# Five edge aggregations of a graph network: windows of eight steps summed in PSUM, and gather buffers released tile by tile

## Chip, cores and metric

The kernel runs on one core of a Trainium2 chip. The metric is the device time of one execution in microseconds; three runs of the kernel before gave 6568.65, 6569.81 and 6577.09 us (median 6569.81).

## What is computed

There are N = 6250 nodes and E = 100000 edges `(src, dst)`, sorted by `dst`, all with 128 features. The distribution of `dst` is skewed: the first nodes have far more edges. Four layers follow each other, each as `x = x + layer(relu(layernorm(x)))`:

```python
# L0: three graph convolutions
norm = dis[src] * ew * dis[dst]
z = relu(segment_sum((z @ W)[src] * norm[:, None], dst, n) + b)      # three times
# L1: out = x + sum of weighted neighbours, then two dense layers
agg = segment_sum(edge_weight[:, None] * x[src], dst, N)
# L2: attention over the edges, with three segment softmaxes
# L3: mean of neighbours
agg = segment_sum(x[src], dst, N) / maximum(deg, 1)
out = agg @ W_l.T + b_l + x @ W_r.T                                  # then each row is normalised
```

So the same aggregation over all edges is done five times ("passes" 0 to 4): pass 0 to 2 for L0, pass 3 for L1, pass 4, after attention, for L3.

## The kernel before

The nodes lie in 49 blocks of 128 (`NB`), the edges in 782 tiles of 128 (`NT`). The table of node rows to be gathered is in HBM, the sums are in SBUF (`AGG`, one column group of 128 per block).

**Steps.** A tile whose edges go to two blocks is worked twice. A "step" is a pair of a tile and a block; there are `PS = NT + NB - 1` = 830 steps, tile and block both grow with the step, and which tile and block a step has depends on the data. `plan_vector` (L1393) works this out at the start, and the engines read it from `plan_reg` into registers, 16 steps at a time (`load_plan`, L508; `load_blocks`, L513; `load_batches`, L1628).

**A pass** has one program per engine, tied together by semaphores:

- POOL, `gathers` (L748): for each tile one indirect DMA of 128 rows of the table into `gath_ring`, which has `RING` = 64 buffers. At every fourth tile it waits on `freed` for the value of `slot_free(t)` (L420). That value holds for any data: since a step's tile can lag behind its number by up to 48, gather t waits for all steps up to t-13.
- SP, `count_batches` (L526): waits until four gathers have landed and counts them in `landed`.
- VectorE, `sums` (L1635): for each step it makes a one-hot matrix (L1661, 128 edges x 128 nodes of the block, times the edge weight), after waiting every fourth step for the batch that has landed; and it adds the product of an earlier step from PSUM into the block of `AGG` whose number is in a register (L1651 or, with a scale per node, L1653). The adds run up to seven steps behind the one-hots (six banks and one, `lead`, L428).
- TensorE, `products` (L904): for each step two matmuls of 128x512 in bf16 whose result nobody reads (`KEEP_BUSY`, L916), then, after waiting for the one-hot, the fp32 product of one-hot and gathered rows (L918) into one bank of PSUM. Every fourth product counts in `freed`, the others in `multiplied`.

**Between passes.** The last 48 steps of a pass carry the next dense layer with them: from step `NT + STAGE_AT` (6) on, TensorE puts in one stage of `dense_stages` (L866: transposes of one group of four blocks, products of the group before) after every fourth step. ScalarE copies the transposes (`dense_copy`, L1163). From step `NT + DRAIN_AT` (13) on, VectorE drains one group at every fourth step (`gcn_drain`, L1283; `gin_drain`, L1297; `gcn_out`, L1288, from `STAGE_AT`; `sage_drain`, L1371). ScalarE stores the group to the table (`keep_rows`, L1145) and starts `AGG` for the next layer with the node's own row times `dis` (`gcn_start`, L1053). There are 13 groups. The gathers of the next pass wait until all groups of the table are stored.

The order of work is written by hand: each engine's list is the order of the Python program, and nothing is reordered.

## Time and profile before

| what | us |
|---|---|
| median of three runs | 6569.81 |
| the profiled execution: its span, the only time given for it | 7709.4 |
| busy: TensorE matmul | 5132.3 (67%) |
| busy: POOL | 4733.2 (61%) |
| busy: VectorE | 3875.4 (50%) |
| busy: ScalarE | 1090.3 (14%) |
| the 7820 keep-busy matmuls (L916) | 2913.7 |
| the 3910 gathers of the passes (L755) | 3731.9 |
| the 4150 one-hots (L1661) | 1420.2 |
| the 4150 adds (L1651, L1653) | 1402.6 |

The profile is of one execution of the program; its times are from the first to the last instruction. "Idle before" is the time that an engine did nothing ahead of an instruction, with what released it: another engine's line, "issue" where nothing in the trace explains it, "remote" where the semaphore's event came from a source that the trace doesn't name. PE is TensorE's matmuls, PEld its weight loads, DVE VectorE, ACT ScalarE, POOL GpSimd, SP the sync engine. A granted clock of 1.0 is 2.4 GHz, 0.5 is 1.2 GHz. The ends of matmuls are modelled.

### The profile page before, as it was taken

How to read it: one execution, taken by the hardware profiler on the slowest of the kernel's cores; microseconds unless marked ns; L12 is line 12 of the kernel's file. 1: busy time of each engine (PE TensorE's matmuls, PEld its weight loads, DVE VectorE, ACT ScalarE, POOL GpSimd, SP SyncE). 2: the span in 40 equal slices, each digit the busy share in tenths (PEclk: the TensorE clock that was granted, in tenths of full speed). 3: DMA queues.
4: the chain of work that ended last, by engine and by line, in shares of the span. 5: the costliest groups of instructions: out<-in, count | busy, mean ns of one | idle time of the engine just before them, and what ended most of it. 6: DMA issues, size and time to landing. Idle time of an engine off the chain costs nothing.

```text
span 7709.4 us, 94745 instructions
## 1 busy us (share of the span) xinstructions
PE 5132.3 (67%) x25896; PEld 3318.3 (43%) x25896; DVE 3875.4 (50%) x11836; ACT 1090.3 (14%) x3004; POOL 4733.2 (61%) x4806
## 2 busy tenths in 40 slices
PE   2666666666666666666566666678888885666666
PEld 1343444444444434344344443545555553344445
DVE  7444444444444444444533333568888876333334
ACT  2000000100000100000100000256666663000001
POOL 7666666566666466666366666366666644666662
PEclk7777777777777777777677777899999997777777
DMA  2211111211111111111111111155555541111111
GB/s 73 54 46 46 46 46 45 54 46 46 46 46 46 50 46 46 46 46 46 43 46 46 46 46 46 44 123 129 129 130 129 129 105 37 46 46 46 46 46 36
DMA packets 384857, 466.38 MB, mean 60 GB/s; under 512 B 103802, under 2 KB 290616, under 8 KB 384326
## 3 DMA queue, kind: packets, MB, share of 16 engines
q0 software_dynamic: 152528, 313.83, 16.4%
q1 hardware_dynamic: 200936, 128.85, 6.8%
q10 hardware_dynamic: 30878, 17.63, 0.8%
q8 instruction: 225, 3.69, 0.2%
q14 instruction: 290, 2.38, 0.1%
HBM read 434.51 MB, written 27.81 MB: 60 GB/s over the span
## 4 chain that ended last, share of the span: by engine, by line
PE 41%; another core or an unknown queue 21%; issue 15%; DVE 12%; POOL 7%; DVEq 2%; ACT 1%; DMA 0%; SPq 0%; ACTq 0%
PE psum L916 14%; PE psum L918 12%; POOL pool L755 7%; DVE work L1653 5%; PE psum L991 3%; PE psum L956 3%; PE psum L967 3%; PE psum L949 2%; DVE pool L1661 2%; PE psum L891 1%; PE psum L942 1%; PE psum L934 1%; DVEq L1653 1%; DVE work L1651 1%
## 5 line engine op out<-in xcount | busy, mean ns | idle before, releaser
L755 POOL DMA_INDIRECT pool<-table,src_col x3910 | 3731.9, 954 | 2112.6 <-issue 1094.4
L918 PE MATMUL psum<-pool 128*128 x8300 | 2109.2, 346 | 2052.0 <-DVE pool L1661 1376.2
L918 PEld LDWEIGHTS psum<-pool 128*128 128x128 f32 x8300 | 1843.5, 240 | 3358.6 <-issue 3030.4
L916 PE MATMUL psum<-busy_rows,iota_b 128*128 128x512 bf16 x7820 | 2913.7, 461 | 24.1 <-issue 23.7
L1653 DVE SCALAR_TENSOR_TENSOR work<-psum,dis,work 128x128 f32 x2490 | 872.8, 351 | 1732.2 <-remote 1240.4
L1661 DVE TENSOR_SCALAR pool<-iota_f,rel_col,ew_col 128x128 f32<-128x128 f32 x3320 | 1173.9, 354 | 384.5 <-issue 301.7
L916 PEld LDWEIGHTS psum<-busy_rows,iota_b 128*128 128x128 bf16 x7820 | 910.3, 117 | 144.1 <-issue 31.6
L727 POOL DMA_INDIRECT gath<-table,src_col x520 | 518.0, 996 | 325.6 <-PE psum L942 205.2
L1653 DVE SCALAR_TENSOR_TENSOR work<-psum,inv_cnt,work 128x128 f32 x830 | 291.3, 351 | 619.8 <-remote 423.2
L1651 DVE TENSOR_TENSOR work<-work,psum 128x128 f32 x830 | 238.5, 287 | 601.7 <-remote 389.1
L727 POOL DMA_INDIRECT ew_col<-table,src_col x312 | 299.7, 961 | 161.9 <-PE psum L942 82.3
L1171 ACT ACTIVATE pool<-psum 128x512 f32<-128x512 f32 (+1 forms) x104 | 56.4, 563 | 2370.8 <-PE psum L878 2370.8
L956 PE MATMUL psum<-pool,weights 128*128 128x512 f32 x416 | 231.0, 637 | 228.8 <-issue 228.8
L1171 ACT ACTIVATE pool<-psum,gcn_bias 128x512 f32<-128x512 f32 (+1 forms) x26 | 17.1, 660 | 2308.1 <-PE psum L878 2308.1
L1661 DVE TENSOR_SCALAR pool<-iota_f,rel_col 128x128 f32<-128x128 f32 x830 | 246.3, 297 | 82.0 <-issue 67.8
L991 PEld LDWEIGHTS psum<-pool,hot 128*128 128x128 f32 x1664 | 208.6, 197 | 179.7 <-issue 174.2
L1685 DVE TENSOR_TENSOR pool<-psum,pool 128x512 f32<-128x512 f32 x208 | 143.2, 689 | 234.9 <-issue 199.3
L991 PE MATMUL psum<-pool,hot 128*128 128x72 f32 x1664 | 239.1, 286 | 9.7 <-DVE work L1755 5.8
L949 PE MATMUL psum<-pool 128*128 128x128 f32 x1664 | 223.2, 278 | 0.0
L967 PE MATMUL psum<-pool,head_sum 128*32 128x512 f32 x1248 | 221.5, 608 | 1.0 <-DVE pool L1690 1.0
L949 PEld LDWEIGHTS psum<-pool 128*128 128x128 f32 x1664 | 205.6, 194 | 0.0
L1191 ACT ACTIVATE pool<-QV 128x128 f32 x832 | 189.7, 298 | 12.7 <-DVE pool L1763 5.6
(221 smaller groups left out, 3769.3 us busy)
## 6 DMA issues: line engine op xcount, KB each, us to landing
pool<-table,src_col POOLq DMA_INDIRECT x3910
pool<-edge_attr SPq DMA_DIRECT2D x832, 64.0 KB
pool<-step_masks SPq DMA_DIRECT2D x624, 48.0 KB
pool<-rel_rows SPq DMA_DIRECT2D x208, 128.0 KB
table<-work ACTq DMA_DIRECT2D x48, 256.0 KB, 2.3
gath<-table,src_col POOLq DMA_INDIRECT x520
ew_col<-table,src_col POOLq DMA_INDIRECT x312
table<-QV SPq DMA_DIRECT2D x12, 256.0 KB, 2.3
```

The costliest lines, as they stand in the source:

```text
L727: gp.indirect_dma_start(out=q_src(n), out_offset=None, in_=table[0][:, :], in_offset=bass.IndirectOffsetOnAxis(ap=src_col[:, s:s + 1], axis=0)
L755: gp.indirect_dma_start(out=gath_ring[:, t % RING, :], out_offset=None, in_=source[:, :], in_offset=bass.IndirectOffsetOnAxis(ap=src_col[: ...
L916: pe.matmul(psum[:, SUM_BANKS, :], iota_b[:, :], busy_rows[:, :], start=True, stop=True)
L918: pe.matmul(psum[:, steps.bank(s), 0:D], hot_ring[:, s % HOT_RING, :], gath_ring[:, bass.ds(slots[s % REGS], 1), :].rearrange("p a d -> p ...
L949: pe.matmul(psum[:, B_QD, j * P:(j + 1) * P], q_block[:, n % SLOT2, :], expand[:, two, j * P:(j + 1) * P], start=True, stop=True).then_inc ...
L956: pe.matmul(psum[:, B_K, :], weights[:, WI["Wk"], :], attr_t[:, g % 2, :], start=True, stop=True).then_inc(keyed, 1)
L967: ins = pe.matmul(psum[32 * kind:32 * (kind + 1), bank, :], head_sum[:, q, :], prod[:, kind, :], start=(q == 0), stop=(q == QUADS - 1), ti ...
L991: ins = pe.matmul(psum[:, B_SUM, q * ACCW:(q + 1) * ACCW].rearrange("p (k i h) -> p k i h", k=3, i=KINDS), hot[:, two * QUADS + q, :], val ...
L1191: act.activation(q_block[:, slot:slot + 1, :], QV[:, bass.ds(blocks[j], 1), :], ACT.Copy).then_inc(block_copied, 1)
L1651: v.tensor_tensor(into, into, part, ALU.add).then_inc(steps.added, 1)
L1653: v.scalar_tensor_tensor(into, part, scale[:, bass.ds(blocks[added % REGS], 1)], into, ALU.mult, ALU.add).then_inc(steps.added, 1)
L1661: v.tensor_scalar(hot_ring[:, s % HOT_RING, :], iota_f[:, :], rel_col[:, s:s + 1], weight[:, s:s + 1] if weight is not None else None, ALU ...
```

## The change

Steps are put together in windows of `WINDOW` = 8 (104 windows). TensorE sums a window's products in two PSUM banks (8 places of 128 columns): it clears them with two zero matmuls of 128x512, adds each product with `start=False` at the place that a register gives (the step's block less the window's first block), closes with two zero matmuls, and counts the window in `done`. It waits for `landed` itself. VectorE makes the one-hots without waiting for `landed`, into 32 buffers, and adds a whole window (128x1024) at once to eight blocks of `AGG`. The scale by `dis` or `inv_cnt` is applied afterwards, a group at a time. The matmuls that kept TensorE busy are gone.

The gather buffers are 48. For each tile the plan holds the window after which the tile is past (`past_i`); ScalarE waits, batch of four by batch, until that window is done, and counts in `slots_free`, on which POOL waits. The plan gets two more columns (place in the window, first block of the window). `STAGE_AT` goes from 6 to 13, `DRAIN_AT` from 13 to 30.

```diff
-        PLAN = 4
+        PLAN = 6
         PS = NT + NB - 1
+        WINDOW = 8
+        NW = ceil_div(PS, WINDOW)
+        TAIL = NT // WINDOW
...
-        FREE = 4
-        RING = 64
-        HOT_RING = 16
-        SUM_BANKS = PS_BANKS - 1
-        KEEP_BUSY = 2
+        RING = 48
+        HOT_RING = 4 * WINDOW
...
-            def slot_free(self, t):
-                steps = t + FREE - 1 - RING + NB - 1 + 1
-                return self.nth * (PS // FREE) + ceil_div(steps, FREE) if steps > 0 else 0
+            def slots_free(self, t):
+                return self.nth * (TILE_BATCHES - NBATCH) + t // BATCH - NBATCH + 1
+        def window_banks(w):
+            return 2 * (w % 4) if w < TAIL else (2, 6)[(w - TAIL) % 2]
+        def window_lead(w):
+            return 3 if w < TAIL + 2 else 2
+        def last_window(g):
+            return min(NW - 1, (NT + groups[g][1] - 2) // WINDOW)
...
+        def release_slots(act, steps):
+            act.wait_ge(past_loaded, 16)
+            last = TILE_BATCHES - NBATCH
+            for j in range(last):
+                if j % REGS == 0:
+                    n = min(REGS, last - j)
+                    first = BATCH * j + BATCH - 1
+                    past = load_plan(mybir.EngineType.Activation, PLAN, first, (n - 1) * BATCH + 1, NW,
+                                     "a tile's last step is one of PS", BATCH, 1)
+                act.wait_ge(steps.done, past[j % REGS])
+                act.sem_inc(slots_free, 1)
...
-        STAGE_AT = 6
-        DRAIN_AT = 13
+        STAGE_AT = 13
+        DRAIN_AT = 30
...
-                if t % FREE == 0 and t >= RING - NB:
-                    gp.wait_ge(steps.freed, steps.slot_free(t))
+                if t % BATCH == 0 and t >= RING:
+                    gp.wait_ge(slots_free, steps.slots_free(t))
...
-            for s in range(PS):
-                if s < NT:
-                    for _ in range(KEEP_BUSY):
-                        pe.matmul(psum[:, SUM_BANKS, :], iota_b[:, :], busy_rows[:, :], start=True, stop=True)
-                pe.wait_ge(steps.hot, steps.before + s + 1)
-                pe.matmul(psum[:, steps.bank(s), 0:D], hot_ring[:, s % HOT_RING, :],
+            for w in range(NW):
+                if window_before(w) is not None:
+                    pe.wait_ge(steps.added, steps.windows_before + window_before(w) + 1)
+                for k in range(2):
+                    pe.matmul(psum[:, window_banks(w) + k, :], iota_b[:, :], zero_rows[:, :], start=True, stop=False)
+                for s in window_steps(w):
+                    if s % REGS == 0:
+                        slots = load_plan(mybir.EngineType.PE, 2, s, REGS, RING - 1, "the plan takes the tile modulo RING")
+                        places = load_plan(mybir.EngineType.PE, 4, s, REGS, WINDOW - 1, "a step goes on by one block at most")
+                        batches = load_batches(mybir.EngineType.PE, s + BATCH - 1)
+                    if s % BATCH == 0:
+                        pe.wait_ge(landed[steps.nth], batches[s % REGS // BATCH])
+                    pe.wait_ge(steps.hot, steps.steps_before + s + 1)
+                    pe.matmul(window_sums(w)[:, bass.ds(places[s % REGS], 1), :].rearrange("p a d -> p (a d)"),
+                              hot_ring[:, s % HOT_RING, :],
+                              gath_ring[:, bass.ds(slots[s % REGS], 1), :].rearrange("p a d -> p (a d)"), start=False,
+                              stop=False)
+                    if s == window_steps(w)[-1]:
+                        for k in range(2):
+                            ins = pe.matmul(psum[:, window_banks(w) + k, :], iota_b[:, :], zero_rows[:, :], start=False, stop=True)
+                        ins.then_inc(steps.done, 1)
...
+            def add_window(a):
+                v.wait_ge(steps.done, a + 1)
+                into = AGG[:, bass.ds(bases[a % REGS], WINDOW), :]
+                v.tensor_tensor(into, into, window_sums(a), ALU.add).then_inc(steps.added, 1)
+                complete = [g for g in range(NGR) if last_window(g) == a]
+                if ready and complete:
+                    v.wait_ge(steps.added, steps.windows_before + a + 1)
+                    for g in complete:
+                        ready(g)
...
+            while added < NW:
+                if drain and added == NW - 1:
+                    stages = (PS - 1 - NT - STAGE_AT) // GROUP + 1
+                    for g in range(drained, stages - 3):
+                        drain(g)
+                    drained = max(drained, stages - 3)
+                add_window(added)
+                added += 1
+            if drain:
+                for g in range(drained, NGR):
+                    drain(g)
...
+            def scale_sums(col):
+                def scale(g):
+                    lo, hi = groups[g]
+                    v.tensor_tensor(AGG[:, lo:hi, :], AGG[:, lo:hi, :], col_bc(col, lo, hi), ALU.mult).then_inc(sums_scaled, 1)
+                return scale
```

`gcn_start` copies a group without the scale in one operation; `gcn_out` (pass 2) begins with the scale. `release_slots` stands in ScalarE's list ahead of the dense copies of each pass. The plan gets one operation over 1x781, two for `past_i`, about eight of 128x7 and one small matmul.

## Rows read from the trace of the kernel before

**Rows 1.** The span and mean granted clock of the only core.
```profile
core 0: 7709.4 us, clock 0.800
```

**Rows 2.** Instructions of line 755 by stretch: start:end, us; POOL busy (count); granted clock; DMA share; GB/s.
```profile
190.40:1319.40 1129.00, 749.79 (x782) 0.77 0.19 47
1319.40:1385.30 65.90, 0.00 (x0) 0.82 0.23 65
1385.30:2510.30 1125.00, 747.09 (x782) 0.76 0.18 46
...
7593.20:7709.40 116.20, 0.00 (x0) 0.75 0.10 29
```

**Rows 3.** Timeline of POOL: start us, us, what, [idle before <-releaser].
```profile
212.00 0.95 POOL L755 DMA_INDIRECT pool<-table,src_col  x1 [0.31 <-issue]
218.75 0.95 POOL L755 DMA_INDIRECT pool<-table,src_col  x1 [5.80 <-PE psum L918]
...
1030.63 0.95 POOL L755 DMA_INDIRECT pool<-table,src_col  x1 [2.38 <-remote]
1031.89 0.95 POOL L755 DMA_INDIRECT pool<-table,src_col  x1 [0.30 <-issue]
```

**Rows 4.** Waits of POOL from 600 to 1400 us: total us, times, longest us.
```profile
POOL pool L755 <- issue: 143.6, 471, 0.3
POOL pool L755 <- remote: 100.7, 41, 2.6
```

**Rows 5.** Timeline, TensorE at the low and then at the full clock.
```profile
1015.46 0.63 PE L918 MATMUL psum<-pool 128*128 x2
...
1015.88 1.06 PE L916 MATMUL psum<-busy_rows,iota_b 128*128 128x512 bf16 x2
...
1016.74 0.63 PE L918 MATMUL psum<-pool 128*128 x2
...
1022.15 0.38 PE L918 MATMUL psum<-pool 128*128 x2
...
1022.81 0.38 PE L918 MATMUL psum<-pool 128*128 x2
```

**Rows 6.** Timeline, a product and the add that takes it.
```profile
1018.01 0.63 PE L918 MATMUL psum<-pool 128*128 x2
...
1025.57 0.35 DVE L1653 SCALAR_TENSOR_TENSOR work<-psum,dis,work 128x128 f32 x1 [4.33 <-remote]
```

**Rows 7.** Timeline behind the last step of the first pass.
```profile
1379.42 0.35 DVE L1653 SCALAR_TENSOR_TENSOR work<-psum,dis,work 128x128 f32 x1 [0.26 <-PE psum L918]
...
1380.80 0.69 DVE L1286 TENSOR_TENSOR work<-psum,dis 128x512 f32<-128x512 f32 x1 [0.44 <-PE psum L891]
...
1381.85 0.69 DVE L1286 TENSOR_TENSOR work<-psum,dis 128x512 f32<-128x512 f32 x1 [0.35 <-PE psum L891]
...
1385.38 0.97 POOL L755 DMA_INDIRECT pool<-table,src_col  x1 [56.87 <-DMA table<-work]
```

**Rows 8.** Attention: one stretch by engine (PE, PEld, DVE, ACT, POOL; clock, DMA); waits of VectorE.
```profile
5150.00:6300.00 1150.00, 942.89 (x6407) 620.45 (x6405) 947.32 (x2244) 737.92 (x2107) 720.36 (x734) 1.00 0.55 129
...
DVE pool L1685 <- issue: 172.3, 136, 2.4
```

**Rows 9.** Groups of the page, VectorE adds of 128x128 and 128x512 with PSUM.
```profile
L1651 DVE TENSOR_TENSOR work<-work,psum 128x128 f32 x830 | 238.5, 287 | 601.7 <-remote 389.1
...
L1685 DVE TENSOR_TENSOR pool<-psum,pool 128x512 f32<-128x512 f32 x208 | 143.2, 689 | 234.9 <-issue 199.3
```

**Rows 10.** Timeline, repeats of a group's first operation: end of third and of last pass.
```profile
3761.90 0.69 DVE L1291 TENSOR_TENSOR work<-work,bias 128x512 f32<-128x512 f32 x1
...
3767.80 0.68 DVE L1291 TENSOR_TENSOR work<-work,bias 128x512 f32<-128x512 f32 x1
...
7697.48 0.68 DVE L1377 TENSOR_TENSOR pool<-psum,bias 128x512 f32<-128x512 f32 x1
...
7701.00 0.69 DVE L1377 TENSOR_TENSOR pool<-psum,bias 128x512 f32<-128x512 f32 x1 [0.77 <-PE psum L891]
```

More of the change, by code:

```diff
@@ L380, in build @@
         dense_sems = [[sem(f"dense_{k}{side}") for k in ("turned", "copied", "multiplied", "drained")] for side in range(2)]
-        pass_sems = [sem(f"pass_{k}") for k in ("hot", "multiplied", "freed", "added")]
+        pass_hot, pass_added = sem("pass_hot"), sem("pass_added")
+        pass_done = [sem(f"pass_done{i}") for i in range(5)]
         class Norm:
@@ L439, in build @@
         q_dense, o_dense = Dense(0, 1), Dense(1, 1)
-        passes = [Pass(i, (7, 6, 2, 3)) for i in range(5)]
+        passes = [Pass(i) for i in range(5)]
         batch_here = [sem(f"batch_here{i}") for i in range(NBATCH)]
@@ L516, in build, with load_batches, load_bases @@
         REGS = 16
+        def load_batches(kind, first):
+            return load_plan(kind, 3, first, REGS - BATCH + 1, ceil_div(NT, BATCH), "the plan takes one more than the batch of a tile", BATCH, 1)
+        def load_bases(first):
+            return load_plan(mybir.EngineType.DVE, 5, first * WINDOW, min(REGS, NW - first) * WINDOW, NB - WINDOW,
+                             "the plan takes the smaller of the block and the last base", WINDOW)
+        def release_slots(act, steps):
[9 more added lines that the diff above has]
+                act.sem_inc(slots_free, 1)
         FIRST_POW = DC // 8
@@ L908, in products @@
             then = list(then)
[L909 to L922 removed]
+            if steps.nth:
+                pe.wait_ge(steps.added, steps.windows_before)
+            else:
+                pe.wait_ge(zeros_made, 1)
+                pe.wait_ge(cols_made, len(COLS))
@@ L1385, in sage_drain @@
                     result(g)
-            sums(v, passes[4], None, inv_cnt, DRAIN_AT, sage_drain)
+            sums(v, passes[4], None, scale_sums(inv_cnt), sage_drain)
         def product_of(g, side=0):
@@ L1399, in plan_vector @@
             v.tensor_copy(row["lb"], fl_block[:, 1, :]).then_inc(own.up(), 1)
+            settle()
+            v.scalar_tensor_tensor(row["fb"][:, 1:NT], row["lb"][:, 0:NT - 1], 1.0, row["fb"][:, 1:NT], ALU.add,
+                                   ALU.min).then_inc(own.up(), 1)
             settle()
@@ L1413, in plan_vector @@
                             ALU.subtract).then_inc(offsets_made, 1)
+            v.scalar_tensor_tensor(past_i, row["off"], float(WINDOW - 1), row["spread"], ALU.add, ALU.add).then_inc(own.up(), 1)
+            settle()
+            v.tensor_scalar(past_i, past_i, WINDOW.bit_length() - 1, None, ALU.arith_shift_right).then_inc(past_made, 1)
             n = 0
@@ L1626, in norm_feed @@
                 norm_end(v, norm, g)
-        def load_batches(first):
-            return nc.values_load_multi_w_load_instructions(
-                plan_reg[3:4, first + GROUP - 1:first + REGS:GROUP], engines=[mybir.EngineType.DVE], min_val=1,
-                max_val=ceil_div(NT, BATCH),
-                skip_runtime_bounds_check_because="the plan takes one more than the batch of a tile")[1]
-        def sums(v, steps, weight, scale, then_at, then, beside=None):
-            v.wait_ge(plan_loaded, 16)
-            added, groups_done = 0, 0
-            for s in range(PS + SUM_BANKS):
-                while added < PS and (s >= PS or added < s - steps.lead(s)):
-                    if added % REGS == 0:
-                        blocks = load_blocks(mybir.EngineType.DVE, added, REGS)
-                    v.wait_ge(*steps.product(added))
-                    if added >= 1:
-                        v.wait_ge(steps.added, steps.before + added)
-                    into = AGG[:, bass.ds(blocks[added % REGS], 1), :]
-                    part = psum[:, steps.bank(added), 0:D].rearrange("p (a d) -> p a d", a=1)
-                    if scale is None:
-                        v.tensor_tensor(into, into, part, ALU.add).then_inc(steps.added, 1)
-                    else:
-                        v.scalar_tensor_tensor(into, part, scale[:, bass.ds(blocks[added % REGS], 1)], into, ALU.mult,
-                                               ALU.add).then_inc(steps.added, 1)
-                    added += 1
-                if s < PS:
-                    if s % REGS == 0:
-                        batches = load_batches(s)
-                    if s % GROUP == 0:
-                        v.wait_ge(landed[steps.nth], batches[s % REGS // GROUP])
```

150 lines of the change are left out of this document (94 added, 56 removed).

## The prediction, made before the change was run

> **What bounds the kernel now.** I looked first at the span and the granted clock of the only core [rows 1]: the traced execution spans 7709.4 us, while the three timed runs have a median of 6569.8 us. The trace is thus 1139.6 us, or 17%, longer than what is to be predicted. So the sum below is made as a difference, in the trace's own durations, and is then put on the median; before that I have to say which part of the traced time exists only in the traced execution.
>
> Next the gather instructions of line 755 by stretch [rows 2]. Each of the five aggregation passes issues its 782 gathers on POOL in 1125 to 1129 us (three of the five rows are left out, they read 1125.0, 1125.0 and 1124.6). Between two aggregation passes no gather is issued for a while (65.9 us in the row shown, the first of three), and 116.2 us follow the last gather. POOL alone has work through a whole pass, so I read its timeline [rows 3]: a gather starts 1.26 us after the one before, 0.95 us of work and 0.30 us of "issue", but every twelfth comes about 2.1 us later than that, after 2.4 us of idle time. The list of waits puts numbers to it [rows 4]: of 513 gathers 41 wait 100.7 us in all for "remote", 2.5 us each. Without these, 782 gathers take 782 x 1.26 = 985 us, 140 us less than the pass shows.
>
> The twelfth gather always waits for the count of finished products (`freed`). With 64 buffers the kernel allows for the worst case of 48 extra steps, so gather t waits until step t-13 is done. TensorE should be far ahead of that: at the full clock a step (two 128x512 matmuls only to keep it busy, and the fp32 product) is 0.65 us, at the low one 1.28 us [rows 5]. But its completions come late. The add at 1025.57 takes the product that was issued at 1018.01, counting both in order; DVE had been idle 4.33 us for it [rows 6]. That closes the ring: late completion, late add (it runs at most seven steps behind), late one-hot, late product, late buffer.
>
> Is this lateness there without the trace? Added up, it would explain the 1139.6 us: five times 140 us = 700 us; the steps left over when the last gather has gone, 60 us from 1319.4 to the last add at 1379.42 [rows 2, 7], where a TensorE that keeps up needs about 6, five times 54 = 270 us; and in attention DVE is busy 947.32 of 1150 us with its first matmul-dependent operation waiting 172.3 us on nothing the trace shows [rows 8], so up to (1150 - 947) x 1340/1150 = 236 us (attention proper lasts about 1340 us, my estimate). Together 1206 us, 66 us more than needed. So I take the passes of the timed runs to be bound by POOL at 1.26 us per gather, with at most 66 us (13 us per pass) of waits left in them. The Trainium skill has a mechanism for it (NOTIFIC — the notification-queue block, "Overflow: three behaviours, one of which stalls the engine": a full record queue can stall the engine that produces the records). No run here shows the queue, only the late completions.
>
> **The change, part by part.**
> *Gathers.* Each issues the same instruction with the same wait on every fourth, now on `slots_free`. A buffer is given back when the last window of its tile is done, at worst 7 steps and 3 tiles late, so POOL may run about 36 tiles ahead instead of 12 at the start of a pass. The wait goes, but what is late next is POOL itself: 985 us per pass before and after. What is certain is one wait: gather 16 of the first pass starts at 218.75 instead of 212.00 + 1.26 = 213.26 [rows 3], because TensorE had not begun; that gives back 5.5 us.
> *TensorE.* The keep-busy pair goes (0.86 us a step at the low clock, 1015.88 to 1016.74), four zero matmuls per window of eight steps come (4 x 0.43/8 = 0.21 us a step), the product stays (0.42 us) [rows 5]. At the low clock a step is 0.63 us against 1.26 x 782/830 = 1.19 us in which its tile arrives. Nothing to gain on the path, nothing to lose. Three register loads per 16 steps instead of one, and the wait for `landed` moved from DVE to TensorE, have 16 x 0.56 = 9 us of room per 16 steps; I take nothing. If that cover failed, each 0.1 us a step beyond it would cost 5 x 83 = 415 us.
> *VectorE.* Eight adds of 0.35 us become one over 128x1024. From 287 ns for 128x128 and 689 ns for 128x512 [rows 9], 1.05 ns an element, it is 1.22 us: 0.15 us a step in place of 0.35. DVE too has room on both sides, so zero.
> *ScalarE* gets the waits and increments that free the buffers, in a stretch where it had nothing; nothing is queued behind them before the first dense copy, and the last release (tile 735) comes before that copy is due. Copying a group of the table without scaling is shorter, but the gathers wait for the stores, not for this copy. Zero. SP counts batches as before.
> *The end of each pass* is where the change adds to the path. Before, after the last add at 1379.42 come four drains, about 1.05 us apart, and the store; the next pass begins at 1385.38 [rows 7]. After: (a) two closing zero matmuls, 0.43 to 0.86 us, I take 0.7; (b) the add of 1.22 for 0.35, +0.9; (c) three groups (10 to 12) are complete only with the last window, and their scaling, 2 x 0.69 + 0.29 and a settle, is 1.8; (d) with `DRAIN_AT` 30 and the rule before the last window only six groups are drained by then, seven are left instead of four: 3 x 1.05 = 3.2. Passes 0 and 1: 6.6 us each, 13.2. Pass 3 has no scaling: 4.8. Pass 2 ends in `gcn_out`, whose first operation is repeated after 5.9 us with four steps of 0.59 between [rows 10], so 3.5 us a group: one group more behind the last add, (a), (b), and three scalings with their settles (2.5) make 7.6. Pass 4 ends in `sage_drain`, 3.5 us apart [rows 10]: 3 x 3.5 + (a) + (b) + (c) = 13.9. Sum 39.5 us. Bounds: 15 us if the drains are covered by waiting for the last tiles, 65 us if these stretches all run at the low clock.
> *Setup.* One operation more over 1x781, some eight of 128x7 and a TensorE round trip. From [rows 9], 0.3 us and up each, partly beside DMA: +3 us, between 0 and 6.
>
> Sum: 39.5 - 5.5 + 3 = +37 us, so 6570 + 37 = 6607 us. In the traced execution the same change removes the late-completion waits too, so there I expect 7709 - 700 - about 200 + 37, about 6850 us.
>
> **The rivals.**
> *Waits are left in the timed passes (faster).* Place: the `freed` wait of every fourth gather. For it: it is the largest wait in the trace, and the 1206 us above rest on an estimate for attention. If attention gives all of its 236 us, 66 us of waits are left: 6570 - 66 + 37 = 6541 us. If the traced 1.26 us of a gather is itself longer than in a timed run, say 1.21, another 3910 x 0.05 = 195 us in the timed passes are waits that go: 6346 us. It decides once more than 37 us are left. Against it: the trace accounts for all the missing time without it, and 1.26 us is the same wherever TensorE is busy or not. Chance 0.32 for anything faster, the greater part of it near 6500 us.
> *The tail is hidden (no change).* If (c) and (d) overlap with waiting for the last tiles and their stores, +15 - 5.5 - 0 is +10 us, 6580 us. Chance 0.20.
> *TensorE stays at the low clock (slower still).* In the passes of before the granted clock is 0.77, alternating between both levels [rows 2]; the keep-busy matmuls go. By the rows the products fit also at 1.2 GHz, but the dense stages behind the last window, five of them at 1.1 us, double: +5.5 us in four passes, 6629 us. Chance 0.08. The Trainium skill warns of just this (TensorE: Matmul & The Clock Gate, Part 1: "the default state is throttled, and activity releases the throttle"); by that rule the change gives up its fast matmuls, by the rows of this pass it can afford to.
> *The release is not exact.* ScalarE frees batches one by one and in order; were it late by more than 36 tiles, POOL would wait again. Nothing in the rows makes it so; within the forecast's chance.
>
> **How the numbers follow.** The forecast, POOL-bound passes and longer ends, has 0.40; slower in all 0.48, faster 0.32, within 0.2% (13 us, about what these runs can tell from no change) 0.20. The range for 8 in 10 reaches down into the first rival and up over the bound of the tails: 6450 to 6650 us. The range of the forecast case alone is 6585 to 6640.
>
> **What would show it.** In the changed kernel's profile: the gathers 1.26 us apart through a whole pass with the "remote" waits gone and about 985 to 990 us per pass; 1.2 us for the window's add; POOL idle between passes for some 20 us; the granted clock of the passes lower. I am wrong if the timed runs fall by more than 37 us, since then waits were left in the passes of before, or a gather was faster than traced; if gathers start further apart than 1.26 us after the change; or if the gather of a pass waits for `slots_free`.

## The result, and the profile after

Eleven runs of the changed kernel have a median of 6555.87 us (6551.84 to 6558.07), eleven of the kernel before 6570.01 us. The ratio is 0.9977, 95% interval 0.9970 to 0.9985: 14 us, or 0.2%, faster where 37 us slower was forecast.

The profiled execution of the changed kernel spans 6553.3 us, the same as its timed runs, while the one of before that the prediction read spans 7709.4 [rows 1]. Its gathers by stretch (line 791; columns as in [rows 2]):

```profile
core 0: 6553.3 us, clock 0.697
193.50:1182.90 989.40, 751.21 (x782) 0.62 0.21 55
1182.90:1201.10 18.20, 0.01 (x1) 0.98 0.57 160
1201.10:2187.50 986.40, 748.34 (x782) 0.61 0.20 54
2187.50:2206.20 18.70, 0.04 (x1) 0.91 0.37 106
...
6498.80:6553.30 54.50, 0.00 (x0) 0.84 0.21 61
```

A pass is 986 us and about 18 us lie between two of the first three passes, as forecast (985 and some 20). The timeline of POOL near gather 16 and the groups of the page show the other forecasts of a size: no wait at gather 16 (in [rows 3] 5.80 us), 1221 ns for the window's add (forecast 1.22 us), and TensorE waiting mostly for landed tiles (1860.7 of 2259.6 us), for one-hots in the rest.

```profile
212.04 0.95 POOL L791 DMA_INDIRECT pool<-table,src_col  x1 [0.30 <-issue]
213.30 0.98 POOL L791 DMA_INDIRECT pool<-table,src_col  x1 [0.30 <-issue]
...
218.46 0.96 POOL L791 DMA_INDIRECT pool<-table,src_col  x1 [0.30 <-issue]
```

```profile
L967 PE MATMUL psum<-pool 128*128 x8300 | 1847.4, 392 | 2259.6 <-SPq L564 1860.7 <-DVE pool L1735 390.7 <-issue 8.0
...
L1725 DVE TENSOR_TENSOR work<-work,psum 128x1024 f32 x520 | 634.7, 1221 | 3155.4 <-PE psum L973 3154.3 <-issue 1.0
```

So the passes are what was said; the sum went wrong elsewhere. To find where, the kernel before had to be traced in an execution that is not 1100 us long.

### The profile page after: what moved, and what is told of

Read it like the earlier page. It is cut to its first block, busy times and chain, and to the rows that moved or that the text cites. A ratio compares the mean times of both kernels' runs of the same rounds, so it can differ in the third digit from the quotient of the medians.

```text
span 6553.3 us, 78540 instructions
## 1 busy us (share of the span) xinstructions
PE 3920.5 (60%) x20158; PEld 2753.8 (42%) x20158; DVE 3125.0 (48%) x8266; ACT 1109.3 (17%) x2896; POOL 4742.9 (72%) x4806
## 4 chain that ended last, share of the span: by engine, by line
POOL 56%; issue 20%; PE 12%; DVE 8%; DMA 2%; SPq 1%; ACT 1%; DVEq 0%; ACTq 0%; POOLq 0%
POOL pool L791 55%; PE psum L1045 2%; PE psum L1021 2%; PE psum L1003 2%; PE psum L1010 2%; PE psum L933 1%; DVE work L1841 1%; PE psum L996 1%; PE psum L988 1%; DMA pool<-table,src_col 1%; PE psum L967 1%; DVE pool L1776 1%; DVE pool L1774 1%; PE psum L1033 1%; PE psum L920 1%
## 5 line engine op out<-in xcount | busy, mean ns | idle before, releaser
L967 PE MATMUL psum<-pool 128*128 x8300 | 1847.4, 392 | 2259.6 <-SPq L564 1860.7
L967 PEld LDWEIGHTS psum<-pool 128*128 128x128 f32 x8300 | 1600.8, 281 | 2770.9 <-issue 2762.6
L1725 DVE TENSOR_TENSOR work<-work,psum 128x1024 f32 x520 | 634.7, 1221 | 3155.4 <-PE psum L973 3154.3
L1735 DVE TENSOR_SCALAR pool<-iota_f,rel_col,ew_col 128x128 f32<-128x128 f32 x3320 | 890.0, 353 | 9.4 <-ACT work L1110 5.5
L973 PE MATMUL psum<-zero_rows,iota_b 128*128 128x512 bf16 x1040 | 521.4, 602 | 0.0
L958 PE MATMUL psum<-zero_rows,iota_b 128*128 128x512 bf16 x1040 | 493.5, 573 | 11.9 <-DVE work L1725 9.0
L958 PEld LDWEIGHTS psum<-zero_rows,iota_b 128*128 128x128 bf16 x1040 | 149.4, 144 | 272.6 <-issue 248.7
L1010 PE MATMUL psum<-pool,weights 128*128 128x512 f32 x416 | 214.1, 596 | 0.0
L1003 PEld LDWEIGHTS psum<-pool 128*128 128x128 f32 x1664 | 203.0, 192 | 0.0
L933 PE MATMUL psum<-weights,pool 128*128 128x128 f32 x980 | 146.6, 300 | 64.2 <-ACT pool L1228 41.2
```

Source lines behind the costliest of these rows:

```text
L933: ins = pe.matmul(psum[:, 4 + 2 * d.side + g % 2, i * P:(i + 1) * P], tr[:, 2 * (k + d.side) + g % 2, i * P:(i + 1) * P], weights[:, WI[w] ...
L958: pe.matmul(psum[:, window_banks(w) + k, :], iota_b[:, :], zero_rows[:, :], start=True, stop=False)
L967: pe.matmul(window_sums(w)[:, bass.ds(places[s % REGS], 1), :].rearrange("p a d -> p (a d)"), hot_ring[:, s % HOT_RING, :], gath_ring[:, b ...
L973: ins = pe.matmul(psum[:, window_banks(w) + k, :], iota_b[:, :], zero_rows[:, :], start=False, stop=True)
L1003: pe.matmul(psum[:, B_QD, j * P:(j + 1) * P], q_block[:, n % SLOT2, :], expand[:, two, j * P:(j + 1) * P], start=True, stop=True).then_inc ...
L1010: pe.matmul(psum[:, B_K, :], weights[:, WI["Wk"], :], attr_t[:, g % 2, :], start=True, stop=True).then_inc(keyed, 1)
```

## Experiments

Six series were run, each beside the kernel before. Four of them had before at 6566 to 6572 us. In the other two (b_ctl, b_keep0, b_exact, b_lead8; later b_banks2, a_gate16) it took 7718 and 7810 us in its timed runs too, so ratios are only taken within a series. Names with b_ are edits of the kernel before, a_ of the changed one. All of them have a bound asserted at run time on the register values that are waited for, which the controls b_ctl and a_ctl have alone.

### Is the lateness of the traced passes a thing of the trace?

**b_ctl**, the control: in `load_batches` the reason for leaving out the bounds check is removed.

```diff
-                max_val=ceil_div(NT, BATCH),
-                skip_runtime_bounds_check_because="the plan takes one more than the batch of a tile")[1]
+                max_val=ceil_div(NT, BATCH))[1]
```

> The kernel before, with only a bound asserted at run time on the batch numbers that VectorE loads from the plan (a control for the edits below). Both theories: within 0.2% of the kernel before (6570 us); its traced execution about 7700 us like before's.

Measured: 7744.5 us, before 7717.8, ratio 1.0031 (1.0019 to 1.0042). The first surprise: before's timed runs are as long as the trace of [rows 1]. The lateness is not added by tracing one execution; a whole series has it or has it not.

**b_keep0**:

```diff
-        KEEP_BUSY = 2
+        KEEP_BUSY = 0
```

> KEEP_BUSY 0: the kernel before without its keep-busy matmuls. Theory T1 (the timed passes of before are bound by POOL at 1.26 us a gather and hold no waits for buffers; the missing 50 us are in the ends of the passes): 6560 to 6585 us. Theory T2 (the timed passes of before hold some 10 us of waits for buffers each, because two keep-busy matmuls and a product, 1.28 us a step at the low clock, are slower than the 1.19 us in which a step's tile arrives): about 6520 us. Both: if the lateness of TensorE's completions in the trace comes from the keep-busy matmuls, the traced span falls from 7709 to within 1% of the timed run; if it comes from something else it stays above 7500 us.

Measured: 7670.5 us, 0.9938 (0.9924 to 0.9952), span 7660. A pass takes 1112 us instead of 1126. So 14 of the 140 us of lateness in a pass go with the keep-busy matmuls, the rest does not come from them.

**b_exact** has the release of the changed kernel alone, counted in fours of steps.

```diff
-                if t % FREE == 0 and t >= RING - NB:
-                    gp.wait_ge(steps.freed, steps.slot_free(t))
+                if t % BATCH == 0 and t >= RING:
+                    gp.wait_ge(slots_free, steps.slots_free(t))
```

> The kernel before with the exact release alone: ScalarE counts each batch of four buffers as free once the last step of its fourth tile is done, 64 buffers, nothing else changed. T1: 6565 to 6580 us (the wait of gather 16 goes, -5.5; two plan operations, +1). T2: about 6520 us. Traced: in it TensorE can be some 50 tiles late, so the waits of every twelfth gather go and the traced passes fall from 1127 us towards 990 us, if lateness is a fixed delay; if TensorE's throughput is what the trace lowers, they stay near 1127 us.

Measured: 7800.1 us, 1.0109 (1.0093 to 1.0124). POOL now runs 64 tiles ahead, its first wait in the second pass is at gather 76 (11 us), and then it waits as before, 2.5 us at every twelfth gather: 1136 us a pass. So it is the rate of the consumers that is low; a delay of fixed length would have been covered.

**b_lead8**:

```diff
-                steps = t + FREE - 1 - RING + NB - 1 + 1
+                steps = t + FREE - 1 - RING + NB - 1 + 1 + 4
```

> The kernel before with POOL held at eight steps ahead instead of twelve (four more steps in the count that a gather waits for). T1 (no waits at 12): a gather of a batch needs 1.26 x 4 + 2.5 us and the step's own work under 2 us, which fits into 8 x 1.26 = 10 us, so at most +20 us (6570 to 6590 us). T2 (waits are there at 12): the lead is already too short and four less adds over 100 us.

Measured: 7728.1 us, 1.0016 (1.0007 to 1.0025). A lead of eight is as good as twelve, even here.

### The same kernels where before takes 6570 us

**a_ctl**, the changed kernel's control (its `load_plan` leaves the check out only where `least` is 0):

> The changed kernel, with only bounds asserted at run time on the batch numbers that TensorE loads and on the release numbers that ScalarE loads (a control), beside the kernel before on the same chip. The runs of the kernel before have shown two speeds, 6570 us and, on the chip of the second series, 7718 us with the same late completions as in the trace of the prediction: so they are no product of tracing. Theory T3: on such a chip a product's completion reaches VectorE some 8 to 10 us late, and the ring of seven banks (one-hot, product, add at most seven steps behind) turns that into 1.4 us a step; the change lets the adds run up to four windows behind, so it takes this loss away: about 6560 us beside 7718 (ratio 0.85). Rival T4: such a chip is slow in something that the changed kernel uses too (matmul issue, semaphores of TensorE in general): then it also takes well over 7000 us. On a chip where before takes 6570 us both say 6555 to 6565 us.

Measured: 6560.3 us, before 6571.6, ratio 0.9983 (0.9974 to 0.9992). Repeats in two more series (**a_ctl2**, **a_ctl3**, same kernel): 6561.7 us, 0.9992 (0.9983 to 1.0001), and 6558.7 us, 0.9989 (0.9980 to 0.9998).

> The changed kernel's control once more, beside the kernel before, on whatever chip this series gets. Where before takes 6570 us: 6560 us again. Where before takes 7718 us (the chip with late completions): T3 (the adds' short ring turns a late completion into a loss) says about 6560 us, ratio 0.85; T4 (slow in what both kernels use) well over 7000 us.

> The changed kernel's control on the chip that this series gets. Where before takes 6570 us: 6560 us. Where before takes 7718 us: T3 about 6560 us, T4 well over 7000 us.

**a_keep2** puts keep-busy matmuls back:

```diff
+                    if s < NT:
+                        for k in range(2):
+                            pe.matmul(psum[:, window_banks(w) + k, :], iota_b[:, :], zero_rows[:, :], start=False, stop=False)
                     pe.wait_ge(steps.hot, steps.steps_before + s + 1)
```

> The changed kernel with two keep-busy matmuls of 128x512 back before each product (zeros added into the window's banks, so the sums stay). T3 and T4: within 0.5% of the changed kernel at a higher granted clock (about 0.8 instead of 0.7), since at 1.2 GHz two of them, a product and a share of four zero matmuls are 0.86 + 0.42 + 0.21 = 1.49 us a step, at 2.4 GHz half of it, against 1.19 us in which a tile arrives. If the granted clock stays near 0.5 the passes are bound by TensorE at 1.49 x 830 = 1237 us and the run takes 1250 us more.

Measured: 6567.0 us, 0.9992 (0.9983 to 1.0001), granted clock 0.96 in a pass instead of 0.62, and the passes last 988 us as without. A higher clock there is worth nothing, since a pass waits for gathers.

**b_banks4** shortens the ring of product and add:

```diff
-        SUM_BANKS = PS_BANKS - 1
+        SUM_BANKS = 4
```

> The kernel before with four banks for products instead of seven, so that the adds run at most four steps behind. T3 (the completion is late by a fixed time and the ring divides it by its depth): on the chip where before takes 7718 us, a pass of 830 steps goes from 1.36 us a step to about 1.36 x 7 / 4 = 2.4 us, and the run to some 11000 us; where before takes 6570 us, at most 7000 us. T4 (a fixed throughput of TensorE): within 2% of before.

Measured: 6575.3 us, 1.0006 (0.9997 to 1.0015); the passes last 978 to 995 us, as in b_ctl2 below.

**a_lead1** adds a window one window later, not three:

```diff
-            return 3 if w < TAIL + 2 else 2
+            return 1
```

> The changed kernel with VectorE adding window w-1 right after the one-hots of window w (one window of slack instead of three). T3: a period holds 8 one-hots (2.9 us), the product's late completion (8 to 10 us) and the add (1.2 us), against 9.5 us in which its tiles arrive and with one window overlapped, so between 0 and 3 us more a window, 6560 to 8000 us on the chip with late completions and 6560 us on one without. T4: 0 to 1% over the changed kernel.

Measured: 6555.5 us, 0.9976 (0.9966 to 0.9986). In both kernels the depth of the ring behind the products is reserve: nothing in a pass needs it. That a_lead1 is 5 us below a_ctl of the same series is within the two intervals.

**b_ctl2** is b_ctl again, for a trace of before's structure that can be set beside a_ctl2 of the same series.

> The kernel before with the asserted bound alone, for a trace of its structure on this chip. On a chip where before takes 6570 us: passes of 986 us with gathers 1.26 us apart and one wait of 7 to 8 us at gather 16 of the first; 15 to 17 us from the last gather of passes 0 and 1 to the next pass (21 in the changed kernel), 36 behind pass 2 (29), 63 behind the last gather of pass 4 (52), as the variant with four banks showed. Its times within 0.2% of before.

Measured: 6573.7 us, 1.0010 (1.0001 to 1.0019): the asserted bound itself costs some 6 us. Its gathers by stretch:

```profile
192.20:1187.10 994.90, 749.08 (x782) 0.86 0.22 56
1187.10:1204.50 17.40, 0.02 (x1) 0.90 0.54 152
1204.50:2190.20 985.70, 747.53 (x782) 0.89 0.21 54
...
3193.90:3231.80 37.90, 0.00 (x0) 0.50 0.20 59
...
6513.00:6577.00 64.00, 0.00 (x1) 0.82 0.18 52
```

and those of a_ctl2, for the same three kinds of stretch (a pass, the end of pass 2, the end of pass 4):

```profile
192.40:1182.10 989.70, 751.55 (x782) 0.64 0.22 55
...
3198.00:3226.00 28.00, 0.00 (x0) 0.60 0.27 80
...
6504.80:6555.70 50.90, 0.04 (x1) 0.80 0.23 65
```

From the starts of the first and last gather of each pass in the two traces comes this account, in us:

| part (gathers are counted from their starts) | before (b_ctl2) | changed (a_ctl2) | difference | forecast |
|---|---|---|---|---|
| up to the first gather | 192.2 | 192.5 | +0.2 | +3 |
| five passes, first to last gather | 4929.4 | 4929.8 | +0.4 | -5.5 |
| of this, the first pass | 993.8 | 988.6 | -5.2 | -5.5 |
| last gather of pass 0 to pass 1 | 18.4 | 19.5 | +1.0 | +6.6 |
| last gather of pass 1 to pass 2 | 16.8 | 21.6 | +4.8 | +6.6 |
| last gather of pass 2 to pass 3 | 39.0 | 29.1 | -9.9 | +7.6 |
| pass 3 to pass 4, attention in it | 1316.2 | 1311.5 | -4.7 | +4.8 |
| last gather of pass 4 to the end ("the last end") | 65.0 | 51.9 | -13.1 | +13.9 |
| span | 6577.0 | 6555.7 | -21.3 | +37 |

The pair overstates the gain: b_ctl2's traced execution is the slowest of its eleven, and the medians of the two differ by 12 us, not 21. Single executions differ by a few us too, so rows of 1 to 3 us say little. The end of pass 2 and the last end say more. Over the traces that keep each kernel's places of stages and drains (b_ctl2, b_keep0b, b_banks4; the changed kernel, its three controls, a_keep2), the first is 36.4 to 39.0 us before and 27.3 to 29.7 us after, the second 62.6 to 65.0 and 51.2 to 55.4. From pass 3 to pass 4 it is 1315.1 to 1316.2 and 1310.4 to 1315.0, which nearly touch. In all three the forecast is wrong in sign.

The forecast was made from the last add of a pass, so each end is cut there (us; for pass 3 the part behind is attention):

| end of pass | last gather to the end of the last add: before, changed | difference | behind it: before, changed | difference | forecast: up to the add, behind it |
|---|---|---|---|---|---|
| 0 | 12.5, 8.0 | -4.5 | 5.9, 11.4 | +5.5 | +1.6, +5.0 |
| 1 | 10.2, 8.2 | -2.0 | 6.7, 13.4 | +6.7 | +1.6, +5.0 |
| 2 | 29.7, 14.9 | -14.8 | 9.2, 14.2 | +5.0 | +1.6, +6.0 |
| 3 | 11.8, 8.1 | -3.7 | | | +1.6, +3.2 |
| 4 | 50.4, 23.8 | -26.6 | 14.5, 28.1 | +13.6 | +1.6, +12.3 |

What follows the last add came out within 2 us of its forecast each time. What stands ahead of it had no term but the closing matmuls and the longer add, 1.6 us, and it became shorter.

**b_keep0b**, again without keep-busy, now beside 6568 us:

> The kernel before without the keep-busy matmuls, as in the second series. On a chip where before takes 6570 us: the passes are bound by POOL, so they stay at 986 us; what the lower clock costs is in the ends of the passes, where transposes and products of the dense layer alternate with VectorE's drains (a round of 16 products took 2.0 us at the high clock, 3.1 to 3.6 us at the low one): 12 to 14 rounds by 1 to 2 us in the last pass, less in the others, so 6585 to 6610 us. If the ends do not depend on the clock: 6570 us.

Measured: 6571.7 us, 1.0007 (0.9998 to 1.0016); in a pass the granted clock is 0.50, one pass 985 us, the last end 62.6 us. The keep-busy matmuls of before were worth nothing. The expected 6585 to 6610 us did not come: no keep-busy matmul stands behind step `NT` (L914, `if s < NT`), and the drains behind the last gather follow each other as in b_ctl2 (10.5, 9.9, 6.7 us in both). So this run does not show what a lower clock in the ends would cost; the rows below do.

### What sets the last ends

The timeline of b_ctl2 behind the last gather of pass 4 (6512.1 us) shows a round:

```profile
6519.63 0.69 DVE L1377 TENSOR_TENSOR pool<-psum,bias 128x512 f32<-128x512 f32 x1 [4.33 <-PE psum L891]
...
6522.69 0.28 DVE L1660 TENSOR_SCALAR pool<-iota_f,rel_col 128x128 f32<-128x128 f32 x1
...
6523.12 0.68 PE L918 MATMUL psum<-pool 128*128 x2 [2.67 <-DVE pool L1660]
...
6523.59 1.91 PE L878 MATMUL psum<-ident,work 128*128 128x128 f32 x8
...
6525.30 2.61 PE L891 MATMUL psum<-weights,pool 128*128 128x128 f32 x16
...
6527.95 0.69 DVE L1377 TENSOR_TENSOR pool<-psum,bias 128x512 f32<-128x512 f32 x1 [3.21 <-PE psum L891]
...
6533.36 0.29 DVE L1660 TENSOR_SCALAR pool<-iota_f,rel_col 128x128 f32<-128x128 f32 x1 [2.26 <-issue]
...
6538.48 0.69 DVE L1377 TENSOR_TENSOR pool<-psum,bias 128x512 f32<-128x512 f32 x1 [3.14 <-PE psum L891]
```

VectorE drains a group (3.1 us) and only then makes the next one-hot; TensorE waits for it, does its products, eight transposes and 16 products, and VectorE waits 3.2 us for these. The two take turns. Behind the last gather the turns of b_ctl2 last 9.4, 8.3, 10.5, 9.9, 6.7 and 7.3 us. No row of this kind stood in the prediction.

**b_late2** begins these turns later:

```diff
-        STAGE_AT = 6
-        DRAIN_AT = 13
+        STAGE_AT = 13
+        DRAIN_AT = 20
```

> The kernel before with the dense stages begun seven steps later (STAGE_AT 13) and the drains too (DRAIN_AT 20), nothing else. Theory T5 (in the last 48 steps of before, VectorE's drain, its one-hots and TensorE's product and dense stage take turns, because a one-hot is made only a few steps ahead, so a group costs 9 to 10 us in the last pass there and 3.5 to 4 us behind the last step): two groups fewer take turns, so 2 x 5.5 = 11 us less in the last pass and some 2 to 4 us less in the others: 6552 to 6560 us where before takes 6570. Rival T6 (the ends of before are set by the gathered tiles or by the groups' own drains, wherever they stand): within 5 us of before, or more, since more groups stand behind the last step.

Measured: 6560.6 us, before 6566.4, ratio 0.9990 (0.9981 to 0.9999); the last end is 49.5 us, 15.5 less than in b_ctl2, pass 3 to pass 4 6.3 less, the ends of passes 0 to 2 up to 3 us longer. The turns are T5's: from the last gather to the last add 28.4 us are left of 50.4, and 6.5 us more stand behind the add (21.0 for 14.5). Two turns fewer are not all of the 22 us: they are also shorter, 6.7 to 6.9 us until the last one of 10.8. Transposes and drains of its last pass, and below them TensorE's busy time and granted clock (0.78 and 1.00) in one stretch of b_ctl2 and one of b_late2:

```profile
6509.90 1.04 PE L878 MATMUL psum<-ident,work 128*128 128x128 f32 x8
...
6512.94 0.68 DVE L1377 TENSOR_TENSOR pool<-psum,bias 128x512 f32<-128x512 f32 x1
...
6519.61 0.69 DVE L1377 TENSOR_TENSOR pool<-psum,bias 128x512 f32<-128x512 f32 x1 [0.32 <-PE psum L891]
...
6526.29 0.69 DVE L1377 TENSOR_TENSOR pool<-psum,bias 128x512 f32<-128x512 f32 x1 [1.56 <-PE psum L891]
```

```profile
6510.20:6548.40 38.20, 22.98 (x130) 0.78 0.17 47
```

```profile
6512.90:6526.30 13.40, 7.75 (x65) 1.00 0.30 85
```

At the full clock the transposes and products of a stage take 3.0 us (1.04 + 1.95), at the low one (1.2 GHz) 5.5 (1.91, and 3.62 in the turn of b_ctl2 from 6510.2 us). Every turn of 6.7 us in the two traces has a granted clock of 1.00; that of 8.3 us has 0.78 and that of 9.4 us 0.65. So the clock is worth 1.6 to 2.8 us a turn. In the turns of 10.5 and 9.9 us it is not all: there VectorE also sits idle for 2.3 and 1.7 us while its registers are loaded from the plan (the 2.26 above, "issue"). Of the 2.3 us about 1.1 is the asserted bound, since the same place in the trace of before, which has none, shows 1.12. Why the clock falls in some turns is not shown: TensorE was busy for 60% of the stretch at 0.78 and for 58% of that at 1.00.

b_late2 has the changed kernel's `STAGE_AT` and nothing else of it, so the whole gain in the last end (13.1 us) can come from the places of stages and drains. That the windows help here besides is not shown. Nor is it for the time as a whole: b_late2 (6560.6 us) and the changed kernel's control in the same series (a_ctl3, 6558.7 us) cannot be told apart. Their ends differ all the same: 39.5 and 29.0 us behind pass 2, 1309.9 and 1315.0 from pass 3 to pass 4, 49.5 and 52.3 for the last end.

The end of pass 2 is another matter: b_late2 leaves it at 39.5 us. There are no dense stages in it; VectorE alone works. In b_ctl2 and then in a_ctl2, the first operations of `gcn_out` (L1291; L1356):

```profile
3205.15 0.68 DVE L1291 TENSOR_TENSOR work<-work,bias 128x512 f32<-128x512 f32 x1
...
3210.71 0.69 DVE L1291 TENSOR_TENSOR work<-work,bias 128x512 f32<-128x512 f32 x1
...
3216.63 0.68 DVE L1291 TENSOR_TENSOR work<-work,bias 128x512 f32<-128x512 f32 x1
```

```profile
3201.52 1.22 DVE L1725 TENSOR_TENSOR work<-work,psum 128x1024 f32 x1
3202.77 0.69 DVE L1356 TENSOR_TENSOR work<-work,dis 128x512 f32<-128x512 f32 x1
...
3206.63 0.69 DVE L1356 TENSOR_TENSOR work<-work,dis 128x512 f32<-128x512 f32 x1
...
3211.85 0.69 DVE L1356 TENSOR_TENSOR work<-work,dis 128x512 f32<-128x512 f32 x1
```

Before, two groups take 11.5 us: 2 x 3.5 and eight times an add and a one-hot (0.6). After, they take 9.1 us: 2 x 3.9 with the scaling and one add of 1.2; the one-hots are made by then (the last 4.8 us ahead of the last gather; before 27 us behind it). It is before's 17 one-hots and their adds behind the last gather, done by VectorE between its groups, that are gone. The reading rests on these rows; no run takes the one-hots' place alone.

**a_lead1_d8** and **a_drain8** drain two groups more ahead of the last window's add, the first with the lead of a_lead1 too:

```diff
-                    for g in range(drained, stages - 3):
+                    for g in range(drained, stages - 1):
                         drain(g)
-                    drained = max(drained, stages - 3)
+                    drained = max(drained, stages - 1)
```

> The changed kernel with one window of slack for the adds instead of three, and with eight groups drained ahead of the last window's add instead of six, so five drains follow it instead of seven. If the ends of the passes are set by the drains behind the last window: 2 x 1.05 us less in passes 0, 1 and 3 and 2 x 3.5 us less in pass 4, so 13 us below the changed kernel (6547 us). If they are set by TensorE's dense stages (which come one group after the other whatever VectorE does): within 3 us of it (6555 to 6560 us).

> The changed kernel with eight groups drained ahead of the last window's add instead of six (half of the edit of a_lead1_d8, the adds keep their three windows of slack). If the drains' place gave all of the 17 us of that variant: 6543 to 6548 us where before takes 6570, the end of pass 4 down from 52 to 42 us. If it needs the shorter lead too (the windows' adds pile up behind the last one-hot, and the drains wait for them): above 6550 us. On the chip where before takes 7718 us: T3 about 6545 us, T4 well over 7000 us.

> The version with one window of slack and eight drains ahead, again, on another chip: ratio to before 0.996 to 0.997 (6544 us where before takes 6570).

Measured: a_lead1_d8 6544.2 us, ratio 0.9964 (0.9951 to 0.9978), last end 41.7 us; in the next series a_drain8 6544.0 us, 0.9960 (0.9947 to 0.9974), last end 43.3 us, and a_lead1_d8b 6538.5 us, 0.9956 (0.9942 to 0.9970), last end 37.1 us. So the place of the drains makes nearly all of it: 9 us in the last end, and the ends of passes 0 and 1 at 17.8 and 15.9 us, as before the change. Both versions beat both kernels: a_drain8 is 26 us below before, and a_lead1_d8 17 below the changed kernel's control in its series (a_ctl2).

Why an earlier drain costs nothing here, when it costs a turn in before, is in the last window's add. In a_ctl2 and then in a_drain8:

```profile
6526.41 1.22 DVE L1725 TENSOR_TENSOR work<-work,psum 128x1024 f32 x1 [6.37 <-PE psum L973]
```

```profile
6517.52 1.22 DVE L1725 TENSOR_TENSOR work<-work,psum 128x1024 f32 x1
```

In a_ctl2 VectorE is idle 6.37 us ahead of this add. In a_drain8 the two more drains fill that time, and the add ends as long after the last gather (24.2 us, 23.8 in a_ctl2). All one-hots are made by then, so TensorE waits for none of these drains. Behind the add 19.1 us are left instead of 28.1: two drains of 2.7 to 3.9 us, and the stretch at the low clock that a_ctl2 has there (granted clock 0.50 for 9 us; 1.00 between the drains of a_drain8).

### Once more where before is long

> The kernel before with two banks for products instead of seven: an add follows its product after one more one-hot. With four banks it was as fast as with seven where before takes 6570 us. One-hot, product and add follow each other in about 0.3 + 0.9 + 0.8 us, two steps at a time, so a step takes about 1.0 us at the high clock and 1.2 us at the low one, against 1.19 us in which its tile arrives. T3 (only the depth of this ring turns late completions into lost time) on a normal chip: 6570 to 6700 us, the passes at 986 us or slightly over; on the chip where before takes 7718 us: (8 to 10 us)/2 a step, over 15000 us. T4: on that chip within 2% of before.

> The changed kernel with one wait more: gather 16 of the first pass waits for the first window, as it waited for the first steps in the kernel before. It prices the one wait that the prediction took as certain (5.5 us given back): first pass 5 to 9 us longer, 6565 to 6570 us where the changed kernel takes 6560; if the wait only moves time from a later one, 6560 us. On the chip where before takes 7718 us: T3 about 6570 us, T4 well over 7000 us.

b_banks2 is b_banks4 with `SUM_BANKS = 2`; a_gate16 adds to `gathers` a wait for `steps.done` of 1 at t = 16 of the first pass. The series had before at 7810.0 us. Measured: b_banks2 8127.2 us, 1.040 (1.0383 to 1.0418), where T3 said over 15000; a_gate16 7700.7 us, 0.9856 (0.9839 to 0.9872), where T3 said 6570. T3 is refuted: a deeper ring does not take the loss away, and the changed kernel has it too, at 1130 us a pass. T4 fits a_gate16 (well over 7000 us), but said within 2% for b_banks2, which lost 4%: with two banks a pass is 1195 us. In that series the change, with this wait added, is worth 109 us; how they divide is open. The price of gather 16 stays with the pair of traces above: 7.96 us of idle time in b_ctl2, none in a_ctl2, 5.2 us between the passes.

## Why the prediction was wrong, point by point

- **The passes, right.** POOL-bound at 1.26 us a gather, 985 us: b_ctl2 984.7 to 986.9 in passes 1 to 3, the change 986.9 to 988.2. The waits of [rows 4] are not in the 6570 us (T1, not T2); b_lead8, b_banks4, a_lead1 and b_keep0b each leave the passes alone. The first rival (waits left, 6541 or 6346 us) is wrong although the time went its way, and the range of 6450 to 6650 us holds the measured 6556 only because it reached down for this rival: that is luck. The forecast case alone was given 6585 to 6640.
- **That the lateness exists only in the traced execution: wrong in its reason.** It belongs to whole series, in timed runs as in traces, and the trace of [rows 2] was of one. The sum was put on 6570 us by an argument that came out right for the passes by taking the late waits out; the bookkeeping of 1206 us had also to guess the ends of before from stretches of 66 and 116 us [rows 2], that are 18 and 65. It came out well all the same: set against b_ctl2, the trace of before is 694 us longer in the passes and 251 from pass 3 to pass 4, 189 in the other four ends (700, 236 and 270 in the bookkeeping, the last for five ends). That the change removes the late waits where they are (6850 us for a traced execution) is wrong: a_gate16 has 1129 to 1134 us a pass and 7700.7 us.
- **Gather 16, -5.5:** the first pass is 5.2 us shorter.
- **TensorE, VectorE, ScalarE, nothing:** held. The clock fell to 0.62 in a pass and cost nothing (a_keep2).
- **The ends, +39.5: the step that failed.** Its terms count only what follows from the last add on: closing matmuls, a longer add, scalings, later drains. Those behind the add were right (+5.5, +6.7, +5.0 and +13.6 us measured for +5.0, +5.0, +6.0 and +12.3). The step put at nothing, without a reason, what the change does to the work between the last gather and the last add: in before 10 to 22 one-hots with the drains between them, which in pass 4 take turns with TensorE and in pass 2 fill VectorE. That work became 14.8 us shorter in pass 2, 26.6 in pass 4 and 2 to 4.5 in the others. With it the ends of passes 0 and 1 are right in sign (+1.0, +4.8 for +6.6 each), those of pass 2 (+7.6, was -9.9), pass 3 (+4.8, -4.7) and pass 4 (+13.9, -13.1) are not. Sum of the last three: +26.3 forecast, -27.7 measured, 54 of the 58 us by which this pair of traces misses the +37 (by the medians of the result it is 51: 6607 for 6556). For pass 4, and with less margin for pass 3, b_late2 shows the cause; for pass 2 only the rows do.
- **Drains moved too far.** Three drains more behind the last add were priced at 3 x 3.5 us in the last pass. Taking two of them back gives 9 us there (a_drain8), so this single term was right in kind.
- **Second rival, tails hidden (6580):** nearest of the slower cases, for the wrong reason. **Third, low clock in the tails:** in before itself it lengthens turns by 1.6 to 2.8 us, and behind the last add of a_ctl2 the clock is 0.50 for 9 us.
- **The signs of being wrong** (over 37 us faster, gathers further apart, waits for `slots_free`) did not show, and yet the sum was wrong: none of them watched the ends.

## What to carry to other kernels

Price the end of a stage from its last unhidden transfer to the next stage's first, with all the work of each engine in it, not from the last operation on. Look there for engines that take turns: a drain put ahead of the operand that the other engine waits for costs both their times, and one put where its own engine would wait costs nothing. Before using a trace, compare its span with the timed runs, and if they differ, do not ask the trace what a wait costs.

## What was not expected of the hardware

In a series where before takes 7718 us, hardly anything that is recorded with a duration is slower: a gather is 954 to 959 ns in all traces, the packets of the gathers' queue have a median of 156 ns in both, and the last of a gather's packets ends 2.2 us after its issue in both. Only TensorE's products are longer, 342 ns on average in b_ctl and 319 in b_ctl2 (1400 to 2500 us), at a granted clock of 0.77 and 0.89. But recorded semaphore events are missing. In the second pass of a_ctl2 I count 13,983 of them, in that of a_gate16 2,860; in the trace of before that the prediction read 4,177, where b_ctl2 has 15,250. With them waits lose their name: VectorE waits mostly for landed tiles in b_ctl2 (L1660), mostly for products in b_ctl (L1652), and most of the latter are "remote". First b_ctl2, then b_ctl, 600 to 1100 us:

```profile
DVE pool L1660 <- SPq L530: 214.6, 91, 3.4
DVE work L1652 <- PE psum L918: 20.2, 25, 1.1
```

```profile
DVE work L1652 <- remote: 172.5, 60, 5.1
DVE work L1652 <- PE psum L918: 61.7, 37, 3.6
```

So "remote" and "issue" in [rows 4, 6] were a sign that records were missing, and in each trace that lacked them the execution was about 1100 us longer or more. One chip showed both: b_late2 and b_banks2 ran on the same chip in two series, with before at 6566 and at 7810 us. The Trainium skill (NOTIFIC — the notification-queue block, "Overflow: three behaviours, one of which stalls the engine") states that a full record queue can drop records or stall the engine. Missing records fit the first and longer executions the second, but the page gives them as different settings of a queue; no run here shows the queue or switches recording off, so the cause stays open, and with it what sets the 1.44 us a gather of these series.
